# Adjacency blocks of a graph layer built from three bf16 products, the blocks of a unit interleaved element by element

## The reference

```python
def _spmm(row, col, val, x):
    return jax.ops.segment_sum(val[:, None] * x[col], row, num_segments=N)
...
h = _spmm(edge_row, edge_col, edge_val, xn)
z = _spmm(edge_row, edge_col, edge_val, h)        # layer 0
A = softmax(z @ W0.T + b0)
z = _spmm(edge_row, edge_col, edge_val, concat([A, A]))   # layer 1
B = softmax(z @ W1.T + b1)
gnn = tanh(concat([A, B]) + h)
x = x + gnn + linear_attention(xn)
x = x + routed_ffn(layernorm(x))                  # 8 experts, capacity 489
```

## Time and profile before

| | |
|---|---|
| runs, us | 1161.41, 1162.5, 1164.13 (median 1162.5) |
| span of the profiled execution, us | 1161.9 |
| PE busy, us (share), instructions | 1097.3 (94%), 4837 |
| PEld busy | 701.6 (60%) |
| DVE busy | 737.1 (63%), 1681 |
| ACT busy | 314.2 (27%) |
| POOL busy | 168.1 (14%) |
| line 1527, 1250 records of 128 or 53 columns | 171.3 us |
| line 1542, 700 records | 291.8 us |
| lines 1073, 1074, 1076 (DVE), 138 each | 91.2, 100.5, 91.1 us |
| HBM | 155 GB/s over the span |

### The profile page before, as it was taken

The page is one execution under the profiler, slowest core; times in us unless marked ns, Lnnn a source line. Parts: engine busy times, 40 slices in busy tenths (PEclk is TensorE's granted clock), DMA queues, the critical chain, the costliest instruction groups (busy, mean ns, idle before and its releaser), DMA issues.

```text
span 1161.9 us, 14112 instructions
## 1 busy us (share of the span) xinstructions
PE 1097.3 (94%) x4837; PEld 701.6 (60%) x4837; DVE 737.1 (63%) x1681; ACT 314.2 (27%) x1038; POOL 168.1 (14%) x206
## 2 busy tenths in 40 slices
PE   5879999999999999999998999999998799999995
PEld 3446666666666666667793444644447666666664
DVE  8989989998786877777760111116788435554444
ACT  4667767421211222122210111101112211122220
POOL 1112223301010100000000000000234511111111
PEclk9899989999999999999998999999999799999998
DMA  5110111123323223343318998997995584555520
GB/s 168 18 45 13 46 47 46 46 91 121 133 96 133 114 112 121 126 154 136 131 57 323 325 354 292 343 343 275 308 320 213 155 217 117 118 141 136 141 63 7
DMA packets 78871, 178.52 MB, mean 154 GB/s; under 512 B 33567, under 2 KB 62011, under 8 KB 66639
## 3 DMA queue, kind: packets, MB, share of 16 engines
q1 hardware_dynamic: 67550, 126.16, 34.1%
q10 hardware_dynamic: 7120, 43.34, 9.2%
q0 software_dynamic: 4128, 8.08, 2.0%
HBM read 116.23 MB, written 63.77 MB: 155 GB/s over the span
## 4 chain that ended last, share of the span: by engine, by line
PE 80%; DVE 9%; SPq 3%; issue 3%; ACT 2%; DMA 1%; POOLq 0%; POOL 0%; ACTq 0%; DVEq 0%
PE ps L1542 21%; PE ps L1691 20%; PE ps L1527 11%; PE ps L1791 10%; PE ps L1779 9%; PE ps L1566 2%; SPq L465 2%; PE ps L1509 2%; PE ps L1442 1%; PE ps L1495 1%; DVE W L1022 1%; SPq L463 1%; DVE XT L1357 1%; ACT W L746 1%; PE ps L1516 1%
## 5 line engine op out<-in xcount | busy, mean ns | idle before, releaser
L1542 PE MATMUL ps<-RING,XX 128*128 128x512 f32 (+2 forms) x700 | 291.8, 542 | 1.0 <-DVE W L1082 1.0
L1691 PE MATMUL ps<-RING,RY 128*128 128x512 f32 (+4 forms) x750 | 273.7, 523 | 5.8 <-issue 5.8
L1691 PEld LDWEIGHTS ps<-RING,RY 128*128 128x128 f32 x750 | 136.8, 196 | 126.4 <-issue 119.0
L1527 PEld LDWEIGHTS ps<-RING 128*128 128x128 f32 x1250 | 164.5, 193 | 40.8 <-issue 34.1
L774 ACT COPY RING<-ps 128x512 f32<-128x512 f32 (+3 forms) x163 | 91.2, 560 | 312.2 <-PE ps L1527 298.2
L1527 PE MATMUL ps<-RING 128*128 128x128 f32 (+1 forms) x1250 | 171.3, 277 | 0.1
L1542 PEld LDWEIGHTS ps<-RING,XX 128*128 128x128 f32 x700 | 118.5, 191 | 68.8 <-issue 60.7
L1073 DVE TENSOR_TENSOR RING<-iota_n,RY 128x512 f32<-128x512 f32 (+1 forms) x138 | 91.2, 661 | 34.5 <-PE ps L1527 31.8
L1074 DVE TENSOR_TENSOR RING<-iota_n,RY 128x512 f32<-128x512 f32 (+1 forms) x138 | 100.5, 728 | 0.0
L1076 DVE TENSOR_TENSOR RING<-RING,RY 128x512 f32<-128x512 f32 (+1 forms) x138 | 91.1, 660 | 0.0
L900 ACT ACTIVATE RY<-ps,b1T 128x489 f32<-128x489 f32 x64 | 42.9, 670 | 172.2 <-PE ps L1779 172.2
(11 more groups left out here) (258 smaller groups left out, 1295.3 us busy)
## 6 DMA issues: line engine op xcount, KB each, us to landing
RING<-adj_dram SPq DMA_DIRECT2D x60, 1280.0 KB, 6.9
adj_dram<-RING ACTq DMA_DIRECT2D x30, 1280.0 KB, 4.5
rbuf_dram<-W SPq DMA_DIRECT2D x8, 516.0 KB, 5.4
RING<-rbuf_dram SPq DMA_DIRECT2D x8, 516.0 KB, 4.0
xbuf_dram<-W SPq DMA_DIRECT2D x8, 512.0 KB, 3.3
XT<-in_L_ffn_w SPq DMA_DIRECT2D x16, 256.0 KB, 5.1
XT<-in_L_ffn_w SPq DMA_DIRECT2D x4, 1024.0 KB, 8.4
RING<-in_L_ffn_w SPq DMA_DIRECT2D x16, 256.0 KB, 4.9
```

Of the source, the lines that this page charges most:

```text
L1527: last = nc.tensor.matmul(o[:, c:c + w], h[:, 0, i, :], h[:, 1, i, 0:w], start=True, stop=(j != s))
L1542: last = nc.tensor.matmul(ps[:, ACC + dd, 0:w], XN[:, j, dd * H:(dd + 1) * H], at[:, i * w:(i + 1) * w], start=(j == 0), stop=True, skip_g ...
L1691: last = nc.tensor.matmul(o, (Y if l == 0 else S0)[:, j, :], RING[:, slot_of[g % 5], i * across + first:i * across + first + w], start=(j ...
```

## The change

From unit index 25 on (the first unit after `LEAD`) a block is the sum of three bf16 products, one for each part of the weight, and the masks are bf16. The roles change: the mask of the first number stays 0 or 1 and is the stationary operand of all three products; the mask of the second number is multiplied by each of the three parts.

- `recs` is bf16 (it was f32). The sum of the three parts, which the first 25 units need, goes to an area of its own, `lead_w`.
- Each of the four buffers holds four planes of bf16: the first mask, three weighted masks and (in the last plane, before the multiply overwrites it) the bare second mask. In a plane the four blocks lie interleaved: element k of block i is at 4k + i (`quad_b`), in units of pairs at 2k + i in two halves (`pair_b`). One block's operand is thus read with a pitch of 8 bytes (4 for pairs).
- DVE makes both masks with one comparison (1024 elements) and the three weighted ones with one multiply (1536). Field values of neighbouring groups lie side by side in `recs`, and a new constant `iota_q` holds each number four times. In units of pairs it is two comparisons (512) and two multiplies (768).
- So that the groups of a strip lie side by side, the extra group moves from place 25 to place 23 (`SPARE`), and tiles 23 and 24 to places 24 and 25 (`place_in`); three iotas on POOL number them instead of one, and the counts in the waits on `s_const` rise by two. A unit of three blocks computes the place of the extra group as its fourth.
- The diagonal block's extra group has buffers of its own, `own_src` and `own_val`: four small DVE operations and three products instead of two and one. In the first 25 units ACT multiplies its weight in, with the others.

```diff
-        recs = RY[:, 0:5 * NG].rearrange("p (f n) -> p f n", f=5)
+        recs = RY[:, 0:1625].bitcast(BF16).rearrange("p (f n) -> p f n", f=5)
+        lead_w = RY[:, 1626:2276]
...
+        hot_b = [h.bitcast(BF16) for h in hot_w]
+        quad_b = [h[:, 0:2048].rearrange("p (a k i) -> p a k i", a=4, i=4) for h in hot_b]
+        pair_b = [h[:, 0:2048].rearrange("p (a c k i) -> p a c k i", a=4, c=2, i=2) for h in hot_b]
+        own_src = [h[:, 2048:2176] for h in hot_b]
+        own_val = [h[:, 2176:2560].rearrange("p (a k) -> p a k", a=3) for h in hot_b]
...
-                    gp.tensor_tensor(w1, w1, w2, ALU.add).then_inc(s_wpart, 1)
+                    gp.tensor_tensor(whole, w1, w2, ALU.add).then_inc(s_wpart, 1)
...
             def gate_constants():
+                v.tensor_scalar(iota_q[:, :].rearrange("p (k a i) -> p a k i", a=2, i=2), ints[:, 160:160 + 2 * P].rearrange("p (k i) -> p k i", i=2).unsqueeze(1).to_broadcast([P, 2, P, 2]),
+                                -1.0 - OWN, None, ALU.add)
...
+                if u == LEAD:
+                    dve.wait_ge(s_recrd, NT)
                 if u < NT * (NS - 1):
...
+                    first = j * NR + s
+                    views = [(quad_b[u % 4], recs[:, :, first:first + 4], iota_q[:, :].rearrange("p (k i) -> p k i", i=4))]
                 else:
...
-                v.tensor_tensor(block(0), every, grid(0), ALU.is_equal).then_inc(s_eq, 1)
-                v.tensor_tensor(block(1), every, grid(1), ALU.is_equal)
+                for h, fields, every in views:
+                    wide = lambda x, m: x.unsqueeze(2).to_broadcast([P, m, P, x.shape[-1]])
+                    last = v.tensor_tensor(h[:, 0:4:3], every.unsqueeze(1).to_broadcast([P, 2, P, fields.shape[-1]]), wide(fields[:, 0:2], 2), ALU.is_equal)
+                last.then_inc(s_eq, 1)
+                for t in own:
+                    i = t * NR + SPARE
+                    v.tensor_scalar(own_src[u % 4], iota_n[:, :], recs[:, 0, i:i + 1], None, ALU.is_equal)
+                    for f in range(3):
+                        v.tensor_scalar(own_val[u % 4][:, f, :], iota_n[:, :], recs[:, 1, i:i + 1], recs[:, 2 + f, i:i + 1], ALU.is_equal, ALU.mult)
                 dve.wait_ge(s_eq, u + 1 - LEAD)
-                v.tensor_tensor(block(0), block(0), grid(2), ALU.mult).then_inc(s_hot, 1)
+                for h, fields, every in views:
+                    last = v.tensor_tensor(h[:, 1:4], h[:, 3:4].to_broadcast([P, 3, P, fields.shape[-1]]), wide(fields[:, 2:5], 3), ALU.mult)
+                last.then_inc(s_hot, 1)
...
             def build(u):
...
+                    for f in range(3):
+                        last = nc.tensor.matmul(o[:, c:c + w], piece(0, i, P), piece(1 + f, i, w), start=(f == 0), stop=(f == 2 and j != s))
                     if j == s:
+                        for f in range(3):
+                            last = nc.tensor.matmul(o[:, c:c + w], own_src[u % 4], own_val[u % 4][:, f, 0:w], start=False, stop=(f == 2))
```

More of the change, by code:

```diff
@@ L34 @@
 EXTRA = NT
+SPARE = 23
 NG = NT * NR
@@ L85, in width, with place_in @@
     return sum(P if t < NT - 1 else LAST for t in tiles)
+def place_in(t):
+    return t if t < SPARE else t + 1
 def strip_with(t):
@@ L216, in graph_program @@
         KC = [ring[:, 5120 + 512 * i:5632 + 512 * i] for i in range(5)] + [RY[:, 5554:6066]]
-        hot = [ring[:, 7680 + 1280 * i:8960 + 1280 * i].rearrange("p (a g n) -> p a g n", a=2, n=P) for i in range(4)]
+        hot_w = [ring[:, 7680 + 1280 * i:8960 + 1280 * i] for i in range(4)]
+        hot = [h.rearrange("p (a g n) -> p a g n", a=2, n=P) for h in hot_w]
+        hot_b = [h.bitcast(BF16) for h in hot_w]
[3 more added lines that the diff above has]
+        own_val = [h[:, 2176:2560].rearrange("p (a k) -> p a k", a=3) for h in hot_b]
         slot_of = [2, 3, 4, 0, 1]
@@ L251, in graph_program @@
         iota_k = sb("iota_k", [P, 2 * P], F16)
+        iota_q = sb("iota_q", [P, 4 * P], BF16)
         thr = sb("thr", [P, NT])
@@ L636, in _ @@
                     w1, w2, w3 = (recs[:, f, j * NR:(j + 1) * NR] for f in (2, 3, 4))
+                    whole = lead_w[:, j * NR:(j + 1) * NR]
                     gp.wait_ge(s_recrd, j + 1)
-                    gp.tensor_tensor(w1, w1, w2, ALU.add).then_inc(s_wpart, 1)
+                    gp.tensor_tensor(whole, w1, w2, ALU.add).then_inc(s_wpart, 1)
                     gp.wait_ge(s_wpart, j + 1)
-                    gp.tensor_tensor(w1, w1, w3, ALU.add).then_inc(s_wsum, 1)
+                    gp.tensor_tensor(whole, whole, w3, ALU.add).then_inc(s_wsum, 1)
                 if it > KV_LAG:
@@ L762, in weigh @@
                 act.wait_ge(s_wsum, u + 1)
-                for i, (j, s) in enumerate(UNITS[u]):
-                    last = nc.scalar.activation(hot[u % 4][:, 0, i, :], hot[u % 4][:, 0, i, :], ACT.Copy, scale=recs[:, 2, j * NR + s:j * NR + s + 1])
+                blocks = list(enumerate(UNITS[u])) + [(4, (j, SPARE)) for j, s in UNITS[u] if j == s]
+                for i, (j, s) in blocks:
+                    last = nc.scalar.activation(hot[u % 4][:, 0, i, :], hot[u % 4][:, 0, i, :], ACT.Copy, scale=lead_w[:, j * NR + s:j * NR + s + 1])
                 last.then_inc(s_wgt, 1)
@@ L1052, in hots @@
                 n, (j, s) = len(b), b[0]
-                h = hot[u % 4]
+                own = [t for t, g in b if t == g]
                 if u < LEAD:
                     dve.wait_ge(s_wsum, u + 1)
[L1056 to L1061, removed]
+                    h = hot[u % 4]
+                    for t in own:
+                        i = t * NR + SPARE
+                        for a in range(2):
+                            v.tensor_scalar(h[:, a, 4, :], iota_n[:, :], recs[:, a, i:i + 1], None, ALU.is_equal)
                     v.tensor_tensor(h[:, :, 0:n, :], iota_n[:, :].unsqueeze(1).unsqueeze(1).to_broadcast([P, 2, n, P]),
@@ L1073, in hots @@
-                v.tensor_tensor(block(0), every, grid(0), ALU.is_equal).then_inc(s_eq, 1)
-                v.tensor_tensor(block(1), every, grid(1), ALU.is_equal)
+                    first = j * NR + s
+                    views = [(quad_b[u % 4], recs[:, :, first:first + 4], iota_q[:, :].rearrange("p (k i) -> p k i", i=4))]
+                else:
+                    views = [(pair_b[u % 4][:, :, t - j], recs[:, :, t * NR + place_in(s):t * NR + place_in(s) + 2], iota_q[:, :].rearrange("p (k i) -> p k i", i=4)[:, :, 0:2]) for t in range(j, j + n // 2)]
@@ L1442, in flip @@
                 return nc.tensor.transpose(dst, src, ident[0:n, 0:n])
-            pe.wait_ge(s_const, 9)
+            pe.wait_ge(s_const, 11)
             pe.wait_ge(s_cnt0, 1)
@@ L1521, in build @@
                 h = hot[u % 4]
+                if u < NT * (NS - 1):
+                    piece = lambda a, i, w: quad_b[u % 4][:, a, 0:w, i]
+                else:
+                    piece = lambda a, i, w: pair_b[u % 4][:, a, i // 2, 0:w, i % 2]
                 ge(pe, s_bev, u - 1)
@@ L1524, in build @@
                 for i, (j, s) in enumerate(UNITS[u]):
-                    c = width(g for _, g in UNITS[u][:i])
+                    c = width(t for _, t in UNITS[u][:i])
                     w = width([s])
-                    last = nc.tensor.matmul(o[:, c:c + w], h[:, 0, i, :], h[:, 1, i, 0:w], start=True, stop=(j != s))
+                    if u < LEAD:
+                        last = nc.tensor.matmul(o[:, c:c + w], h[:, 0, i, :], h[:, 1, i, 0:w], start=True, stop=(j != s))
+                        if j == s:
+                            last = nc.tensor.matmul(o[:, c:c + w], h[:, 0, 4, :], h[:, 1, 4, 0:w], start=False, stop=True)
+                        continue
+                    for f in range(3):
+                        last = nc.tensor.matmul(o[:, c:c + w], piece(0, i, P), piece(1 + f, i, w), start=(f == 0), stop=(f == 2 and j != s))
                     if j == s:
-                        last = nc.tensor.matmul(o[:, c:c + w], h[:, 0, 4, :], h[:, 1, 4, 0:w], start=False, stop=True)
+                        for f in range(3):
+                            last = nc.tensor.matmul(o[:, c:c + w], own_src[u % 4], own_val[u % 4][:, f, 0:w], start=False, stop=(f == 2))
                 last.then_inc(s_bmm, 1)
```

18 lines of the change are left out of this document (7 added, 11 removed).

## The result

The changed kernel takes 1218.6 us (1217.47 to 1219.88, four runs) against 1162.5: 1.048 of the time before, with a 95% interval of 1.0466 to 1.0495. It is 56 us slower where 20 us of gain were forecast.

What follows compares the result with a forecast made beforehand. PE's matmul issue was taken to bound the graph stage, with DVE having slack. Product gains of 21.5 us less 1.5 for diagonal units gave 20 us, so 1162.5 becomes 1142 us, range 1131 to 1166.

Steps and rivals of the forecast that it cites:

- The bound: Graph stage: matmul issue on PE sets the pace (busy 347.8 of 348 us in 232 to 580 us); DVE has slack.
- Products at 0.0606 us: New bf16 products on PE: 0.0606 us each, so twelve take 0.727 us against 0.89 in f32; 16.3 us gained in fours.
- a sign of being wrong: Builds in the profile after: the forecast is wrong if twelve products take 0.89 us or more.
- The upper bound named: New bf16 products: at 0.11 us each, the price of an f32 record, the loss is some 65 us.
- a product costs more than 74 ns: Rival at the new bf16 products, read at 8 bytes: slower, 1174 us at 81 ns, some 65 us lost at 0.11; chance 0.11.
- The 81 ns of the Trainium skill: Weight load and 128-column matmul streams: said to sustain about 81 ns each; twelve would take 0.97 us, more than f32.
- Pairs: Builds of pair units: 0.83 us becomes 0.727, 0.10 us gained a unit, 1.3 us over 12.5 units.
- Masks on DVE: Compare and multiply per unit on DVE: 0.60 and 0.87 us (0.65 and 0.93 long), 1.60 with the wait; covered by PE.
- they go one element at a time: Rival at DVE's compare and multiply: 1.14 and 1.68 us, DVE sets the pace, 50 us more, 1212 us; chance 0.08.
- DVE binds in places: Rival in units of three and pairs: wide DVE operations 15% slower make PE wait, gain only 10 us, 1152; chance 0.12.
- The 1.5 us taken off for the diagonal units: Diagonal units at 232 to 261 us: extra small DVE operations hold PE back, so 1.5 us is deducted from the gain.
- The rest at nothing: Iotas, first stage, waits, PSUM copies and block stores cost nothing; everything behind the stage moves by the whole gain.

Runs made afterwards that it cites:

- e1: Changed kernel with TensorE reading operands of units 25 to 124 at eleven pairs of pitches, nine units each (blocks not the adjacency); one run, 1224.9 us, read by its trace.
- e2: Changed kernel with TensorE reading both operands at 4 bytes in all units, VectorE still writing four interleaved (blocks of fours and threes not the adjacency); ratio 0.982 to the kernel before.
- e3: Changed kernel with two blocks interleaved, written and read so, in all units from index 25 on, values unchanged; 1150.6 us, ratio 0.985 to the kernel before.

## Why the prediction was wrong

**The bound (right).** PE's issue in the graph stage bounds both kernels, and what a build costs goes into the time one to one: 56 us worked out of the rows, 56.1 between the medians.

**Products at 0.0606 us (wrong; this is the step that failed).** It was taken from line 1495, of the "same type, size, loads and nearly the same layout". The difference that "nearly" passed over, a pitch of 8 bytes for 4, doubles the price: 117 ns (117 in e1, 115 with only the moving operand at 8 bytes). Twelve of them take 1.40 us, past the 0.89 us that the prediction gave as a sign of being wrong. The row itself was read rightly, as was its use for a pitch of 4: the quad builds of e2 and e3 give 58. The upper bound named, 0.11 us and some 65 us of loss, is near where the change landed, yet the range ended at a product of 76 ns. The choice of 61 ns rested on likeness, where the trace had no row at that pitch, and the Trainium skill's two accesses to a line, which 8 bytes "just meets", did not warn of it. The rival had a chance of 0.11.

**The rival "a product costs more than 74 ns" (it came true).** Its point and its far price held (12 x 117 ns is 1.40 us). Its far sum of 65 us is above the 56 because it priced the pairs and the diagonal blocks as dear too, and these are read at pitches of 4 and 2 bytes and became cheaper. Its mechanism was half right: it named both operands, and e1 shows that the stationary one has hardly a part in it, 2 ns of the 59. The 81 ns of the Trainium skill ("TensorE: Matmul & The Clock Gate", Back-to-back issue gap) are not seen at either pitch: 56 to 64 ns with the moving operand at 2 or 4 bytes, 115 to 120 at 8.

**Pairs.** Forecast 0.10 us of gain a unit, measured 0.33: products of 53 columns cost less than those of 128, where 61 ns were taken for all. With 58 ns for the six wide ones, 0.50 us leaves about 26 for each of the six of 53 columns.

**Masks on DVE (right).** 0.69 and 0.96 us against 0.65 and 0.93; the rival that they go one element at a time fell with these rows. The rival that DVE binds in places is not tested by the change, where PE is slower than forecast: its chain has 7 us of masks, at the change to pairs, as that of e2 has, and the kernel before has 7 us there too. With the shorter mask operations of e3 it came in part (24 us of the chain, and the 2.9 us by which its stretch is longer than that of e2).

**The 1.5 us taken off for the diagonal units (not spent).** Neither the change nor e2 has a wait of PE for DVE between 222 and 262 us; e3, with more operations on DVE, has 1.8 us.

**Left out.** No step had a dearer apply. In the change that is 0.015 us a unit, 2 us. With the pitch of 4 bytes (e2, e3) it is 0.05 us for units of four and three and 0.02 for pairs, 6.5 us, and there it is offset: builds of 0.69 and 0.52 us instead of 0.73 and 0.55 (4.4 us) and the pairs (3 us).

**The rest at nothing (right).** The first stage reads the same, and the gain or loss of the stage goes to the end: 56.5 us in the stretch, 56.1 in the time. With the pitch of 4 bytes, the stretch shrinks by 19.9 us in e3 and 22.8 in e2, where 20 were forecast. That nearness is in part luck: the terms above that were missed on either side cancel.

## What to carry to other kernels

Before an operand is interleaved for VectorE's sake, look at what TensorE then reads: by these runs, in bf16 the elements of the moving operand may lie up to 4 bytes apart, in f32 up to 8, and those of the bf16 stationary one up to 32 at some 6 ns (no more was tried). Interleaving by two already gives VectorE its two elements at a time (0.53 ns an element in lines 1018 and 1022); four gave no more an element (0.53) and cost 59 ns a product. And where the only unmeasured thing about an operation is its access pattern, keep its far bound in the range: a row that is "nearly" the same says nothing of a limit between it and the new one.

## What the runs showed of the hardware

- The price of a bf16 product of 128 columns is nearly flat up to a moving pitch of 4 bytes (56, 58 ns), rises by 28 ns on average for every 2 bytes up to 16, and is nearly flat from there (225, 225, 230).
- The stationary pitch adds 0 to 2 ns to a bf16 product at 8 bytes and 5 to 8 at 16 and 32 (62 against 56), but nearly doubles an f32 record at 16 bytes (218 against 111).
- Two f32 matmuls of 512 columns (an apply) take longer the shorter the products in front are: 1.77 us behind bf16 products of 58 ns, 1.74 behind 88 ns, 1.73 from 115 ns on, 1.72 behind f32 records of 111 ns.
